# Local attention with 160 keys per 32 queries, P in DRAM rows of nine blocks, Q and K sent together

## The chip, the cores and the metric

The kernel runs on one core of a Trainium2 chip. The metric is the device time in microseconds of one execution, the median of the runs shown; the profiled execution has a time and a span of its own.

## What is computed

Two blocks follow each other. The first is an RWKV-like attention over x of shape (2, 4096, 256) (stages "mix", "scan" and "gate" of the kernel); the change does not touch it. The second, which the change touches, is a transformer of two layers with local attention. Per layer:

```
q, k, v = split(shift_token(x) @ wqkv)          # 8 heads of 64
q, k    = rotary_xpos(l2norm(q) * qs, l2norm(k) * ks)
# windows of 128 tokens, each looks at its own and the one before
sim  = (8 q) . k;   mask = (i < j) | (i > j + 128) | (j == -1)
attn = softmax(where(mask, -max, sim));  o = attn @ v
x = x + o @ wo
x = x + mlp(layernorm(shift_token(x)))          # a * gelu(g), 2 x 682 hidden
```

A query i sees the keys j with i - 128 <= j <= i, at most 129 of them. In a window of 128 queries the kernel before computes 256 scores per query, the window's own keys and those of the window before, and masks what is too far or in the future.

## The kernel before

All five engines run one long program by hand-written order and semaphores, stage after stage. `local_stage` is the last. It works in windows of P = 128 tokens. There are two batches ("streams" s = 0, 1), 32 windows each and two layers, thus units u = 0..63 per stream and 128 **halves**: `half(s, u, w, l)` does, on each engine, the attention of stream s in window u up to P (scores, softmax, transposes), and, for the other stream o, the rest of its window um (values, output projection, layer norm, MLP). w is the parity of u; it names the one of two buffers that holds the window's K and V. A head pair hp = 0..3 is two heads, which lie in partitions 0..63 and 64..127 of q and k, transposed; pairs 0, 1 are group g = 0 and pairs 2, 3 group 1.

Everything is float32. A float32 matmul shows as two MATMUL records.

**PE** (the `half` at L2582) issues per half, in this order: values of pairs 0 and 1 of the other stream (`values`, L2516), scores of pairs 0 and 1 (`scores`, L2498), values of pairs 2, 3, scores of pairs 2, 3, `project_out` (L2524), the K projection of the next window (L2473), `mean` (L2529), V projection, `variance` (L2533), Q projection, and the MLP (L2551, L2559). In layer 1 `turn_out` (L2567) stands between the first two score pairs and the second values. `scores` has two matmuls per pair, one per head: 64 rows of weights (q of 128 queries) against 256 keys. They go to PSUM banks lB and lC for an even pair, to lA of both streams for an odd one, and pairs 2 and 3 wait until VectorE has read pairs 0 and 1 (`Q["mx"]`).

**VectorE** adds the mask and takes the row maximum (`row_max`, L2186, L2193), ScalarE exponentiates (L2367), GpSimd divides by the row sum (`normalise`, L2033) and VectorE transposes P in 32x32 blocks (`turn_p`, L2202), two pairs for a write. In VectorE's order `deviate` (L2228), which subtracts the mean of the other stream's layer norm, stands ahead of `inverse_sums(s, u, 3)` and of all four `turn_p`; `turn_k` (L2158) lies between the second and the third `turn_p`, `turn_q` (L2152) near the end of the half. For window 0 of a layer the mask of the keys before is all masked; `remask` (L2213) puts it back.

**DRAM round trips.** A block transpose only turns 32x32 blocks. The blocks change places by a write to DRAM and reads back, all issued on SP's queue: `write_q` (L1891) and `read_q` (L1899), `write_k` (L1907) and `read_k` (L1915), and, per group, `write_p` (L1924) and `read_p` (L1932). A write is one transfer of 128 rows; a read is four, one for each 32 target partitions. SP's order in a half is: reads of Q, the store or load of windows, write P group 0, write K, write P group 1, read P group 0, read K, read P group 1, write Q. SP issues in this order, and each wait holds back what stands behind it. `values` of pair 2 wait for the reads of P's group 1.

```
def read_p(s, u, g):
    ...
    for j in range(BL):
        sp.dma_start(pT[s][32 * j:32 * j + 32, g].rearrange("p i h x t -> p i (h x t)"),
                     a["pz"][s, g].rearrange("(i c) (j n) -> j c i n", i=BL, j=BL)[j])...
```

In the gate stage, `load_y` reads its tokens from DRAM with the pattern `"o t c b g h i -> (o c) t (b g h i)"`, where o is 1 and c 8: 8, then 16, then 512 elements, into 128 partitions (L1524). It is not changed; the prediction counts its packets.

Of the kernel before, what the change touches and what calls it, by code (L numbers as in the profile page):

```python
# [21 lines left out]
ALU = mybir.AluOpType  # L22
# [3 lines left out]
P = 128  # L26
NB = 2
# [1718 lines left out]
def local_stage(nc, persist, a, T):  # L1746
# [7 lines left out]
    BL = P // 32  # L1754
    rows, const, ident = (persist[k] for k in ("rows", "const", "ident"))
    wqkv, wo, w1, w2, b1c, lngb, qks = (persist[k] for k in ("wqkv", "wo", "w1", "w2", "b1c", "lngb", "qks"))
    G = ((0, 1), (2, 3), (4, 5))
    with ExitStack() as ctx:
# [3 lines left out]
        wm = one("wm", [P, 2 * P])  # L1762
        mean_w, pause, least = one("mean_w", [P, P]), one("pause", [P, NB]), one("least", [P, 1])
        x1s, dsqs = two("x1s", [P, P]), two("dsqs", [P, P])
        mask = [two(f"mask{s}_", [P, 2, P]) for s in range(NB)]
# [15 lines left out]
        sems = {n: ctx.enter_context(nc.semaphore(f"l_{n}")) for n in ("wm", "set", "prep", "zero", "free", "wqkv", "wo", "w1", "w2", "wiped0", "wiped1")}  # L1781
        R = signals(nc, ctx, "tab", 1, "lr")
        S = signals(nc, ctx, "q_ps k_ps v_ps qsq ksq v_sb ss_q ss_k clamped ln_n rn rq8 kn qm qr k12 kr q_turned k_turned "
                    "q_out:16 k_out:16 qT:64 kT:64 mask0 wo_ps carry x1 x1_sum mean_ps dev dsq dsq_sum var_ps ln_v rstd hn w2_ps hout "
# [61 lines left out]
        def scored(s, hp, x):  # L1846
            return ((bank[s][1], bank[s][2]), (bank[s][0], bank[1 - s][0]))[hp % 2][x][:, 0:2 * P]
# [4 lines left out]
        with nc.Block() as block:  # L1852
            @block.sync
            def _(sp):
# [30 lines left out]
                def write_q(s, u):  # L1885
# [3 lines left out]
                    sp.wait_ge(S["qT"][s].sem, S["qT"][s].after(u, 1))  # L1889
                    sp.sem_inc(sems["free"], 1)  # L1890
                    sp.dma_start(a["qz"][s], q1[s][:].rearrange("p h d -> p (h d)")).then_inc(S["q_out"][s].sem, 16)  # L1891

                def read_q(s, u):
                    sp.wait_ge(S["q_out"][s].sem, S["q_out"][s].after(u))
                    sp.sem_inc(sems["free"], 1)
                    sp.wait_ge(Q["sc"][s].sem, Q["sc"][s].after(u * NHP - 1))
                    sp.sem_inc(sems["free"], 1)
                    for j in range(BL):
                        sp.dma_start(qT[s][32 * j:32 * j + 32].rearrange("p (i t) h -> p i (t h)", i=BL),  # L1899
                                     a["qz"][s].rearrange("(i c) (j n) -> j c i n", i=BL, j=BL)[j]).then_inc(S["qT"][s].sem, 16)  # L1900

                def write_k(s, u):
                    sp.wait_ge(S["k_turned"][s].sem, S["k_turned"][s].after(u))
                    sp.sem_inc(sems["free"], 1)
                    sp.wait_ge(S["kT"][s].sem, S["kT"][s].after(u, 1))
                    sp.sem_inc(sems["free"], 1)
                    sp.dma_start(a["kz"][s], k1[s][:].rearrange("p h d -> p (h d)")).then_inc(S["k_out"][s].sem, 16)  # L1907

                def read_k(s, u, w):
                    sp.wait_ge(S["k_out"][s].sem, S["k_out"][s].after(u))  # L1910
                    sp.sem_inc(sems["free"], 1)
                    sp.wait_ge(Q["sc"][s].sem, Q["sc"][s].after(u * NHP - 1))
                    sp.sem_inc(sems["free"], 1)
                    for j in range(BL):
                        sp.dma_start(kT[s][32 * j:32 * j + 32, w].rearrange("p i h t -> p i (h t)"),  # L1915
                                     a["kz"][s].rearrange("(i c) (j n) -> j c i n", i=BL, j=BL)[j]).then_inc(S["kT"][s].sem, 16)
# [850 lines left out]
```

## Time and profile before

| what | us |
|---|---|
| median of 3 runs (lowest, highest) | 4970.12 (4965.47, 4972.37) |
| profiled execution, its own time | 4966.22 |
| its span | 4964.4 |
| PE busy, share of the span | 4507.8, 91% |
| VectorE busy | 3564.7, 72% |
| ScalarE busy | 2979.7, 60% |
| GpSimd busy | 2441.6, 49% |
| mean granted TensorE clock | 0.959 |

An engine's busy time is the time in which at least one of its instructions runs; issuing a transfer is not counted. PE's matmuls are pipelined and their ends are modelled, so the start of the next one tells more than a length. The mean length of a matmul record holds its latency; what a record costs in a stream is busy time divided by count. For a transfer the profile gives the time from issue to landing. "SPq" is the queue on which SP issues, "PEld" the weight loads. A row's bracket tells the idle time before it and what ended it.

### The profile page before, as it was taken

Reading aid. Unit: us, or ns where it says so; the run is one execution under the profiler, and the core shown is the slowest. Engines: PE = TensorE matmul, PEld = TensorE weight load, DVE = VectorE, ACT = ScalarE, POOL = GpSimd, SP = SyncE. Lnnn points to the kernel's source line nnn. Section 1 sums busy time; section 2 is a strip of 40 time slices with the busy share of each in tenths; the row PEclk is TensorE's granted clock in tenths of the full one; section 3 lists DMA queues with packets and bytes.
Section 4 is the critical chain, followed back from the end, with each engine's and each line's share of the span. In section 5 each row is a group of like instructions: output and inputs, shape, how many; then the busy total and the mean of one; then the engine's idle time right before and its main releaser. Section 6 shows DMA issues by size and latency. Waiting matters only on the chain. (4 is left out here: it accounts for less than half of the span.)

```text
span 4964.4 us, 269505 instructions
## 1 busy us (share of the span) xinstructions
PE 4507.8 (91%) x107928; PEld 3817.4 (77%) x107928; DVE 3564.7 (72%) x10345; ACT 2979.7 (60%) x8486; POOL 2441.6 (49%) x3196
## 2 busy tenths in 40 slices
PE   7898898678888888666999999999999999999998
PEld 6888888678888888654777777777777777777777
DVE  4666666568878887475777777777777777777775
ACT  5777777534444444354666666666666666666665
POOL 1222222267777777203555555555555555555554
PEclk8999999789999999788999999999999999999999
DMA  2343343467777777694555666555565555555554
GB/s 87 87 96 93 93 98 89 114 143 165 165 165 163 167 164 161 175 299 126 170 170 168 173 174 171 172 171 171 180 196 175 173 173 172 171 171 173 173 175 131
DMA packets 1283528, 775.96 MB, mean 156 GB/s; under 512 B 686800, under 2 KB 1179088, under 8 KB 1282256
## 3 DMA queue, kind: packets, MB, share of 16 engines
q1 hardware_dynamic: 1231888, 700.43, 53.1%
q10 hardware_dynamic: 51392, 73.02, 5.0%
q14 instruction: 190, 1.56, 0.1%
q8 instruction: 58, 0.95, 0.1%
HBM read 410.44 MB, written 362.68 MB: 156 GB/s over the span
## 5 line engine op out<-in xcount | busy, mean ns | idle before, releaser
L2367 ACT ACTIVATE l_prob<-l_prob,l_nb,l_rq 128x256 f32<-128x256 f32 x1024 | 601.6, 590 | 20.8 <-DVE l_nb L2193 13.1
L2033 POOL TENSOR_TENSOR l_prob<-l_prob,l_rinv 128x512 f32<-128x512 f32 x512 | 526.8, 1039 | 108.4 <-DVE l_rinv L2173 108.4
L2017 POOL TENSOR_TENSOR l_k<-l_kn,l_tab 128x512 f32<-128x512 f32 x128 | 162.5, 1270 | 614.8 <-DVE l_kn L2165 614.8
L2559 PE MATMUL lD<-l_hid,w 128*128 128x128 f32 x3072 | 364.0, 275 | 0.0
L2559 PEld LDWEIGHTS lD<-l_hid,w 128*128 128x128 f32 x3072 | 353.3, 192 | 0.0
L2551 PEld LDWEIGHTS lA<-l_hn,w 128*128 128x128 f32 x2048 | 242.9, 195 | 110.1 <-POOL l_hn L2051 61.1
L2202 DVE STREAM_TRANSPOSE l_pb<-l_prob 128x512 f32<-128x512 f32 x512 | 326.6, 676 | 0.6 <-POOL l_prob L2033 0.5
L2027 POOL TENSOR_TENSOR l_qr<-l_q 128x512 f32<-128x512 f32 x128 | 162.4, 1269 | 328.1 <-DVE l_q L2131 328.1
L1097 POOL TENSOR_TENSOR sc_aqx<-sc_late,sc_headmask 128x256 f32<-128x256 f32 x256 | 170.8, 667 | 278.9 <-PE sc_Y L1190 277.2
L1173 PE MATMUL sc_AB<-sc_aq,sc_bkx 32*32 32x32 f32 x16384 | 257.3, 198 | 37.4 <-POOL sc_bkx L1097 29.1
L497 POOL TENSOR_TENSOR rk<-rk,bkraw 128x256 f32<-128x256 f32 x64 | 54.6, 871 | 477.9 <-DVE bkraw L383 477.9
L2551 PE MATMUL lA<-l_hn,w 128*128 128x128 f32 x2048 | 266.0, 284 | 11.8 <-POOL l_hn L2051 5.2
L1115 POOL TENSOR_TENSOR sc_bkT<-sc_tok,sc_headmask 128x128 f32<-128x128 f32 x512 | 263.2, 534 | 0.0
L2524 PE MATMUL lD<-l_oT,wo 128*128 128x128 f32 x2048 | 262.6, 281 | 0.1
L2524 PEld LDWEIGHTS lD<-l_oT,wo 128*128 128x128 f32 x2048 | 238.2, 191 | 29.2 <-issue 28.9
L2473 PE MATMUL lB<-wqkv,l_h 128*128 128x512 f32 x512 | 242.9, 597 | 17.4 <-DVE l_mask L2262 17.2
L2551 PE MATMUL lB<-l_hn,w 128*128 128x128 f32 x2048 | 250.9, 276 | 0.0
L1173 PEld LDWEIGHTS sc_AB<-sc_aq,sc_bkx 32*32 32x32 f32 x16384 | 213.3, 108 | 39.4 <-issue 38.6
L2473 PE MATMUL lC<-wqkv,l_h 128*128 128x512 f32 x512 | 241.0, 593 | 0.0
L2473 PE MATMUL lA<-wqkv,l_h 128*128 128x512 f32 x512 | 240.9, 593 | 0.0
L2551 PEld LDWEIGHTS lB<-l_hn,w 128*128 128x128 f32 x2048 | 240.5, 193 | 0.0
L2193 DVE TENSOR_TENSOR l_nb<-l_mx,l_nrq 128x2 f32<-128x2 f32 x512 | 220.6, 431 | 17.7
(276 smaller groups left out, 13707.3 us busy)
## 6 DMA issues: line engine op xcount, KB each, us to landing
scratch_pz<-l_pb SPq DMA_DIRECT2D x256, 512.0 KB, 3.0
l_pT<-scratch_pz SPq DMA_DIRECT2D x1024, 128.0 KB, 3.2
scratch_cm<-cm SPq DMA_DIRECT2D x64, 512.0 KB, 4.1
scratch_qz<-l_q SPq DMA_DIRECT2D x128, 256.0 KB, 2.9
l_qT<-scratch_qz SPq DMA_DIRECT2D x512, 64.0 KB, 2.0
scratch_kz<-l_k SPq DMA_DIRECT2D x128, 256.0 KB, 2.8
l_kT<-scratch_kz SPq DMA_DIRECT2D x512, 64.0 KB, 2.9
sc_early<-scratch_cm ACTq DMA_DIRECT2D x59, 512.0 KB, 4.7
```

What stands on the lines that cost most here:

```text
L1097: return nc.gpsimd.tensor_tensor(dst[:], src.unsqueeze(2).broadcast_to([P, 2 * BG, HQ, CH]), headmask[:].unsqueeze(1).unsqueeze(3).broadca ...
L1115: last = nc.gpsimd.tensor_tensor(bkT[c % 2][:, b * BG:(b + 1) * BG], tok[k][:, c, b, 1:3].rearrange("p x g i -> p (x g) i").unsqueeze(2) . ...
L1173: last = mm(AB_ps[c][at, (x * BG + q) * QH:(x * BG + q + 1) * QH], bkx[c][at, 2 * q + x].rearrange("p h t -> p (h t)"), aq[c][at, q], star ...
L2017: tt(k1[s][:], kn[s][:], wide(2, slice(0, DH)), ALU.mult)
L2033: tt(prob[s][:, pair], prob[s][:, pair], rinv[s][:, pair].unsqueeze(2).broadcast_to([P, 2, 2 * P]), ALU.mult).then_inc(Q["pn"][s].sem, 1)
L2193: tt(nb[s][:, pair], mx[s][:, pair], nrq8[s][:, pair], ALU.mult).then_inc(Q["nb"][s].sem, 1)
L2202: nc.vector.transpose(pb[s][:, g, :, at:at + 2].rearrange("p j h x t -> p (h x) j t"), prob[s][:, 2 * hp:2 * hp + 2].rearrange("p h (x j k ...
L2367: last_ = nc.scalar.activation(prob[s][:, h], prob[s][:, h], ACT.Exp, scale=rq8[s][:, h:h + 1], bias=nb[s][:, h:h + 1], accum_out=sums[s][ ...
L2473: last_ = mm(bank[s][j][:], h[:, k * P:(k + 1) * P], wqkv[:, k, j * INNER:(j + 1) * INNER], start=(k == 0), stop=(k == CC - 1))
L2524: last_ = mm(bank[s][3][:, m * P:(m + 1) * P], wo[:, k, m * P:(m + 1) * P], oT[s][:, k], start=(k == 0), stop=(k == NHP - 1))
L2551: last_ = mm(bank[s][j][0:MW, at:at + P], w1[:, k, tile * MW:(tile + 1) * MW], hn[s][:, k], start=(k == 0), stop=(k == CC - 1))
L2559: last_ = mm(bank[s][3][:, c * P:(c + 1) * P], w2[:, m, c * P:(c + 1) * P], hid[s][:, m], start=(c == 0 and m == 0), stop=(c == CC - 1 and ...
```

## The change

- **Scores.** Queries are taken in blocks of 32. Each block sees five blocks of 32 keys, its own and the four before it, 160 keys. `scores` has 8 matmuls per pair (4 blocks, 2 heads), each with 64x32 weights and 160 columns, into the 32 partitions of its block. For this K of the window before must lie directly ahead of K of this one: qkT has three places of four blocks; even windows use place 2 with place 1 ahead, odd windows place 1 with place 0 ahead, so the K of an even window is also read into place 0 (four more transfers, L1913 of the changed file).
- **Masks.** One mask of 160 columns per row, and one for the first window of a layer; `remask` and the mask copies at the start fall away. Row maxima, exponentials and normalisation work on 160 columns.
- **Q and K** are transposed into one buffer, written by one transfer (512 KB) and read by four of 128 KB, at the place where K was. Reads and write of Q of their own fall away.
- **P** has five blocks per row of 32 queries. Its DRAM buffer has rows of nine blocks per query block, filled with zeros once at the start; the write puts five blocks where they belong, and the reads take eight, so that the blocks that no score was made for are read as zeros. The write is 320 KB, its DRAM side is 4 x 32 x 640 elements; reads are 8 runs of 128 elements per partition where they were 4 of 256.
- On PE and SP each wait is followed by an increment of a spare semaphore (`free_pe`, `free`).
- At the start GpSimd clears qkT (3072 elements per partition) and pT (2048) for each stream where it cleared kT (1024) and a mask (256).
- The words of the change also name "deviation first on VectorE"; in the code `deviate` keeps its place between `inverse_sums` 2 and 3.

```diff
+    NR = BL + 1
+    SPAN = 32 * NR
+    PITCH = 40
...
-        qT, kT = two("qT", [P, P, NHP]), two("kT", [P, 2, BL, NHP, 32])
-        V, prob = two("V", [P, 2, HEADS, DH]), two("prob", [P, HEADS, 2 * P])
-        pb, pT = two("pb", [P, 2, BL, NHP, 2, 32]), two("pT", [P, 2, BL, NHP, 2, 32])
+        qk, qkT = two("qk", [P, BL, 2, NHP, 32]), two("qkT", [P, 3 * BL, 2, NHP, 32])
+        V, prob = two("V", [P, 2, HEADS, DH]), two("prob", [P, HEADS, SPAN])
+        pb, pT = two("pb", [P, 2, NR, NHP, 32]), two("pT", [P, 2, BL, 2, NHP, 32])
...
+                def write_qk(s, u):
...
+                    sp.dma_start(a["qkz"][s], qk[s][:].rearrange("p j y h t -> p (j y h t)")).then_inc(S["qk_out"][s].sem, 16)
...
+                def read_qk(s, u, w):
...
+                    turned = a["qkz"][s].rearrange("(i c) (j n) -> j c i n", i=BL, j=BL)
+                    cur = (2, 1)[w] * BL
                     for j in range(BL):
-                        sp.dma_start(kT[s][32 * j:32 * j + 32, w].rearrange("p i h t -> p i (h t)"),
-                                     a["kz"][s].rearrange("(i c) (j n) -> j c i n", i=BL, j=BL)[j]).then_inc(S["kT"][s].sem, 16)
+                        sp.dma_start(qkT[s][32 * j:32 * j + 32, cur:cur + BL].rearrange("p i y h t -> p i (y h t)"),
+                                     turned[j]).then_inc(S["qkT"][s].sem, 16)
+                    if w == 0:
+                        for j in range(BL):
+                            sp.dma_start(qkT[s][32 * j:32 * j + 32, 0:BL, 1].rearrange("p i h t -> p i (h t)"),
+                                         turned[j][:, :, 32 * NHP:]).then_inc(S["kT"][s].sem, 16)
...
-                    sp.dma_start(a["pz"][s, g], pb[s][:, g].rearrange("p j h x t -> p (j h x t)")).then_inc(H[g]["p_out"][s].sem, 16)
+                    n = 32 * NHP
+                    sp.dma_start(bass.AP(a["pz"].tensor, (s * 2 + g) * 32 * PITCH * n + (BL - 1) * n,
+                                         [[(2 * BL + 1) * n, BL], [PITCH * n, 32], [1, NR * n]]),
+                                 pb[s][:, g].rearrange("p r h t -> p (r h t)")).then_inc(H[g]["p_out"][s].sem, 16)
...
-                        sp.dma_start(pT[s][32 * j:32 * j + 32, g].rearrange("p i h x t -> p i (h x t)"),
-                                     a["pz"][s, g].rearrange("(i c) (j n) -> j c i n", i=BL, j=BL)[j]).then_inc(H[g]["pT"][s].sem, 16)
+                        start = (s * 2 + g) * 32 * PITCH * n + (j + BL - 1) * n
+                        sp.dma_start(pT[s][32 * j:32 * j + 32, g].rearrange("p i x h t -> p (i x) (h t)"),
+                                     bass.AP(a["pz"].tensor, start, [[PITCH * n, 32], [BL * n, 2 * BL], [1, n]])
+                                     ).then_inc(H[g]["pT"][s].sem, 16)
...
-                        for t in (kT[s], V[s]):
+                        for t in (qkT[s], V[s], pT[s]):
                             nc.gpsimd.memset(t[:], 0.0)
...
-                                                               in1=mask[s][w][:].rearrange("p x n -> p (x n)"), scale=1.0, scalar=3 * MASKED,
+                                                               in1=wm[:, int(u in (0, NW))], scale=1.0, scalar=3 * MASKED,
...
-                    for x in range(2):
-                        rows_ = slice(x * DH, (x + 1) * DH)
-                        last_ = mm(scored(s, hp, x), qT[s][rows_, :, hp], kT[s][rows_, :, :, hp].rearrange("p x i t -> p (x i) t"),
-                                   start=True, stop=True)
+                    own, back = (2, 1)[w] * BL, (1, 0)[w] * BL
+                    for i in range(BL):
+                        for x in range(2):
+                            rows_ = slice(x * DH, (x + 1) * DH)
+                            last_ = mm(scored(s, hp, x)[32 * i:32 * i + 32], qkT[s][rows_, own + i, 0, hp],
+                                       qkT[s][rows_, back + i:back + i + NR, 1, hp], start=True, stop=True)
...
-                            last_ = mm(valued(s, hp)[x * DH:(x + 1) * DH], V[s][:, slot, 2 * hp + x], pT[s][:, g, :, at + x, slot],
+                            last_ = mm(valued(s, hp)[x * DH:(x + 1) * DH], V[s][:, (1 - w, w)[slot], 2 * hp + x], pT[s][:, g, :, slot, at + x],
```

How the order of the transfers moves on SP's queue, in one half of layer 0. Before (shapes are those of the target; x4 means four in a row):

```order
L1899 DMA l_qT<-scratch_qz 32x4x128 x4
L1883 DMA scratch_h<-l_hout 256x1x128
L1861 DMA l_h_0<-scratch_h 128x2x129
L1924 DMA scratch_pz<-l_pb 128x1024
L1907 DMA scratch_kz<-l_k 128x512
L1924 DMA scratch_pz<-l_pb 128x1024
L1932 DMA l_pT<-scratch_pz 32x4x256 x4
L1915 DMA l_kT<-scratch_kz 32x4x128 x4
L1932 DMA l_pT<-scratch_pz 32x4x256 x4
L1891 DMA scratch_qz<-l_q 128x512
```

The same place after the change, in a half of the kind that also copies K (the other kind lacks L1913):

```order
L1885 DMA scratch_h<-l_hout 256x1x128
L1868 DMA l_rot<-in_rotary 128x256
L1863 DMA l_h_1<-scratch_h 128x2x129
L1923 DMA scratch_pz<-l_pb 4x32x640
L1898 DMA scratch_qkz<-l_qk 128x1024
L1923 DMA scratch_pz<-l_pb 4x32x640
L1935 DMA l_pT<-scratch_pz 32x8x128 x4
L1909 DMA l_qkT<-scratch_qkz 32x4x256 x4
L1913 DMA l_qkT<-scratch_qkz 32x4x128 x4
L1935 DMA l_pT<-scratch_pz 32x8x128 x4
```

Q's reads and write are gone from the two ends, K's place now carries both, and four transfers more stand ahead of the last reads of P. The write of P is 4x32x640 where it was 128x1024.

On PE the scores of pairs 0 and 1 and the values around them, before:

```order
L2516 MATMUL lD<-l_pT,l_V 64x128 x8
L2498 MATMUL lB<-l_kT,l_qT 128x256
L2498 MATMUL lC<-l_kT,l_qT 128x256
L2498 MATMUL lA<-l_kT,l_qT 128x256 x2
L2516 MATMUL lB<-l_pT,l_V 64x128 x8
```

and after:

```order
L2512 MATMUL lD<-l_pT,l_V 64x128 x8
L2494 MATMUL lB<-l_qkT 32x160
L2494 MATMUL lC<-l_qkT 32x160
L2494 MATMUL lB<-l_qkT 32x160
L2494 MATMUL lC<-l_qkT 32x160
L2494 MATMUL lB<-l_qkT 32x160
L2494 MATMUL lC<-l_qkT 32x160
L2494 MATMUL lB<-l_qkT 32x160
L2494 MATMUL lC<-l_qkT 32x160
L2494 MATMUL lA<-l_qkT 32x160 x8
L2512 MATMUL lB<-l_pT,l_V 64x128 x8
```

Four matmuls have become sixteen small ones; what stands around them is the same.

## Rows read from the trace of the kernel before

**Rows 1.** Windows: busy time by engine, clock, DMA share, GB/s; gate and local stage.
```profile
core 0: us, PE busy (x) PEld busy (x) DVE busy (x) ACT busy (x) POOL busy (x), PEclk, DMA share, GB/s
2100.00:2200.00 100.00, 65.21 (x304) 52.71 (x303) 70.83 (x190) 54.90 (x152) 0.00 (x0) 0.88 1.00 299
2500.00:3400.00 900.00, 897.19 (x6524) 697.66 (x6523) 667.59 (x2271) 598.36 (x1635) 492.31 (x551) 1.00 0.59 171
```

**Rows 2.** Timeline of PE and DVE, one half: start us, us, what.
```profile
3026.08 0.60 PE L2498 MATMUL lB<-l_kT,l_qT 64*128 64x256 f32 x1
...
3027.32 1.09 PE L2516 MATMUL lB<-l_pT,l_V 128*64 128x128 f32 x16
3028.34 0.60 PE L2498 MATMUL lB<-l_kT,l_qT 64*128 64x256 f32 x1
...
3029.95 2.05 PE L2524 MATMUL lD<-l_oT,wo 128*128 128x128 f32 x16
...
3033.56 0.38 PE L2529 MATMUL lD<-l_x1s,l_mean_w 128*128 128x128 f32 x2
...
3047.85 0.88 PE L2516 MATMUL lB<-l_pT,l_V 128*64 128x128 f32 x12
...
3033.98 0.42 DVE L2228 TENSOR_TENSOR l_dev<-l_x,lD 128x256 f32<-128x256 f32 x1 [1.38 <-PE lD L2529]
...
3034.39 1.28 DVE L2202 STREAM_TRANSPOSE l_pb<-l_prob 128x512 f32<-128x512 f32 x2
```

**Rows 3.** Windows of line L2524 alone, in layer 1.
```profile
3850.00:4850.00 1000.00, 98.48 (x768) 89.33 (x768) 1.00 0.59 173
```

**Rows 4.** Timeline of SP's queue, the same half.
```profile
3032.71 0.60 SPq L1861 DMA_DIRECT2D l_h<-scratch_h  x1
3035.84 0.34 SPq L1924 DMA_DIRECT2D scratch_pz<-l_pb  x1
3036.44 0.34 SPq L1907 DMA_DIRECT2D scratch_kz<-l_k  x1
3037.62 0.32 SPq L1924 DMA_DIRECT2D scratch_pz<-l_pb  x1
3038.73 1.82 SPq L1932 DMA_DIRECT2D l_pT<-scratch_pz  x4
3040.74 1.73 SPq L1915 DMA_DIRECT2D l_kT<-scratch_kz  x4
3042.64 1.74 SPq L1932 DMA_DIRECT2D l_pT<-scratch_pz  x4
```

**Rows 5.** DMA from 2600 to 3200 us; issues: count, size, us to landing.
```profile
DMA packets 102611, 101.68 MB, mean 169 GB/s; under 512 B 10544, under 2 KB 87728, under 8 KB 102576
...
q1 hardware_dynamic: 102576, 101.39, 59.2%
...
scratch_pz<-l_pb SPq DMA_DIRECT2D x59, 512.0 KB, 2.7
l_pT<-scratch_pz SPq DMA_DIRECT2D x232, 128.0 KB, 3.2
...
l_rot<-in_rotary SPq DMA_DIRECT2D x15, 128.0 KB, 2.6
```

**Rows 6.** Waits from 3000 to 4000 us: total, times, longest.
```profile
PEld lA L2498 <- DVE l_mx L2186: 10.6, 39, 0.3
...
PEld lB L2516 <- DMA l_pT<-scratch_pz: 9.9, 15, 1.6
```

**Rows 7.** Windows of L2559 and of L2516 alone; a group of the scan stage.
```profile
3000.00:4000.00 1000.00, 139.32 (x1176) 135.26 (x1176) 1.00 0.60 176
3000.00:4000.00 1000.00, 107.23 (x1568) 83.58 (x1568) 1.00 0.60 176
L1173 PEld LDWEIGHTS sc_AB<-sc_aq,sc_bkx 32*32 32x32 f32 x1586 | 20.3, 104 | 0.0
```

**Rows 8.** Timeline at the start of the local stage, POOL and PE.
```profile
2256.95 0.95 POOL L2069 MEMSET l_kT<- 128x1024 f32 x1 [225.59 <-POOLq L104]
...
2264.14 3.78 PE L2473 MATMUL lB<-wqkv,l_h 128*128 128x512 f32 x4 [17.17 <-DVE l_mask L2262]
```

**Rows 9.** DMA of the gate stage, 2103 to 2203 us.
```profile
DMA packets 28640, 30.02 MB, mean 300 GB/s; under 512 B 1683, under 2 KB 21349, under 8 KB 28640
...
ga_gr<-scratch_gr SPq DMA_DIRECT2D x19, 512.0 KB, 8.0
scratch_xa<-ga_xa SPq DMA_DIRECT2D x19, 256.0 KB, 7.8
ga_xt<-in_x SPq DMA_DIRECT2D x19, 256.0 KB, 8.0
scratch_h<-ga_h SPq DMA_DIRECT2D x38, 128.0 KB, 6.4
ga_yt<-scratch_y_tok SPq DMA_DIRECT2D x19, 256.0 KB
```

**Rows 10.** DMA from 3036.7 to 3037.9 us, within a write of P.
```profile
DMA packets 119, 0.49 MB, mean 406 GB/s; under 512 B 0, under 2 KB 0, under 8 KB 119
...
q1 hardware_dynamic: 119, 0.49, 100.9%
```

**Rows 11.** The page, part 6: issues over the whole execution.
```profile
scratch_pz<-l_pb SPq DMA_DIRECT2D x256, 512.0 KB, 3.0
```

More of the change, by code:

```diff
@@ L1761, in local_stage @@
         rot, tab = two("rot", [P, 4, DH]), two("tab", [P, 4, DH])
-        wm = one("wm", [P, 2 * P])
+        wm = one("wm", [P, 2, SPAN])
         mean_w, pause, least = one("mean_w", [P, P]), one("pause", [P, NB]), one("least", [P, 1])
         x1s, dsqs = two("x1s", [P, P]), two("dsqs", [P, P])
-        mask = [two(f"mask{s}_", [P, 2, P]) for s in range(NB)]
         hT = [two(f"h{s}_", [P, CC, P + 1]) for s in range(NB)]
@@ L1940, in first @@
                     sp.dma_start(wm[:], a["winmask"]).then_inc(sems["wm"], 16)
[L1941 to L1945 removed]
+                    sp.wait_ge(sems["set"], 1)
+                    for s in range(NB):
+                        for g in range(2):
+                            sp.dma_start(a["pz"][s, g], pT[s][:].rearrange("p g i x h t -> p (g i x h t)")[:, 0:PITCH * NHP * 8]
+                                         ).then_inc(sems["blank"], 16)
+                    write_qk(0, 0)
+                    read_qk(0, 0, 0)
+                    sp.wait_ge(sems["blank"], 16 * 2 * NB)
                 def half(s, u, w, l, mlp=True):
@@ L2181, in row_max @@
                     dve.wait_ge(Q["p_turned"][s].sem, Q["p_turned"][s].after(n, NHP))
-                    if hp == 0 and w == 0:
-                        dve.wait_ge(S["mask0"][s].sem, S["mask0"][s].after(u, 1))
                     nc.vector.memset(pause[:, s:s + 1], 0.0)
@@ L2259, in first @@
                     dve.wait_ge(sems["set"], 1)
-                    for s in range(NB):
-                        nc.vector.tensor_copy(mask[s][0][:, 0, :], wm[:, P:2 * P])
-                        last = nc.vector.tensor_copy(mask[s][1][:].rearrange("p x n -> p (x n)"), wm[:])
-                    last.then_inc(sems["prep"], 1)
-                    dve.wait_ge(sems["prep"], 1)
                     for s in range(NB):
@@ L2587, in half @@
                     if mlp:
-                        values(o, um, 0, layer(um, l))
-                        values(o, um, 1, layer(um, l))
+                        values(o, um, wm_, 0, layer(um, l))
+                        values(o, um, wm_, 1, layer(um, l))
                     scores(s, u, w, 0)
@@ L2594, in half @@
                     if mlp:
-                        values(o, um, 2, layer(um, l))
-                        values(o, um, 3, layer(um, l))
+                        values(o, um, wm_, 2, layer(um, l))
+                        values(o, um, wm_, 3, layer(um, l))
                     scores(s, u, w, 2)
@@ L2624, in last @@
                     for hp in range(NHP):
-                        values(s, u, hp, 1)
+                        values(s, u, w, hp, 1)
                     turn_out(1 - s, u)
@@ L2707, in lay_out @@
     out["eye16"] = np.ascontiguousarray(np.broadcast_to(np.eye(CH, dtype=np.float32), (P, 2, CH, CH)))
-    q, kx = np.arange(P)[:, None], np.arange(P)[None, :]
-    neg = np.float32(MASKED)
-    before, own = np.where(kx < q, neg, 0), np.where(kx > q, neg, 0)
-    out["winmask"] = np.concatenate([before, own], axis=1).astype(np.float32)
+    row, r = np.arange(P)[:, None], np.arange(160)[None, :]
+    neg, behind = np.float32(MASKED), r - row % 32
+    near = np.where((behind < 0) | (behind > P), neg, 0)
+    begin = np.where(r < P - row // 32 * 32, neg, near)
+    out["winmask"] = np.stack([near, begin], axis=1).astype(np.float32)
     n = out["x"].shape[1]
```

90 lines of the change are left out of this document (34 added, 56 removed).

## The prediction

> **What bounds the kernel now.** I read the windows by stage first. In the local stage (from about 2260 us to the end, 2.7 of the 4.96 ms, and the only stage that the change touches) PE is busy over 99% of the time at granted clock 1.00, with DVE at 74%, ACT at 66%, POOL at 55% and DMA at 59% [rows 1]. So PE bounds this stage, or something lies so close behind it that PE hardly waits. The timeline of one half shows which. On PE the values of head pairs 2 and 3 (L2516, to lB) start at 3027.32 and in the next half at 3047.85 [rows 2]: a half takes 20.5 us in layer 0. In layer 1, 768 records of L2524, 16 to a half, in 1000 us make 20.8 us [rows 3].
>
> Then I follow what those values wait for, the chain that goes through DRAM. Values at 3027.32, scores of pairs 2 and 3, L2524, a projection, the mean at 3033.56; DVE's deviation at 3033.98 and, behind it on DVE, the transposes of P at 3034.39; SP's first write of P at 3035.84, the K write, the second write of P at 3037.62, four reads of P, four of K, and the four reads of group 1 of P from 3042.64 on [rows 2, 4]. The last of those four is issued near 3044.0 and lands a median 3.2 us later [rows 5], at about 3047.2; PE wants it at 3047.85. **This loop has about 0.6 us of slack in 20.5.** The waits agree: PE's weight load for these values already waits for the DMA 15 times in 1000 us, 9.9 us in all [rows 6]. Two loops thus run almost level, PE's own and the one through DRAM, and the change touches both.
>
> **The change, part by part.**
>
> Scores. A head pair has now 2 matmuls of 64x128 weights and 256 columns; after it has 8 of 64x32 and 160. Now two pairs take 1.24 us (3026.08 to 3027.32) and the second two 1.61 us (3028.34 to 3029.95), of which part is the wait for the row maxima, 10.6 us in 39 cases of 1000 us [rows 2, 6]. The trace has no 64x32 tile. Below: a record of 128 columns costs 139.32/1176 = 118 ns at full array [rows 7], so 160 columns cost 0.15 us, two records per matmul 0.3 us, if all eight tiles run side by side. Above: the four column groups in turn, 1.2 us per pair. The nearest row is L2516, where two 64-column tiles over the same 128 rows make 1568 records in 107.23 us, 68 ns each [rows 7]: column groups that share rows do run side by side. I take 0.4 us per pair, thus 0.8 for pairs 2 and 3 (minus 0.8) and 0.8 for pairs 0 and 1 (minus 0.4). The added waits' increments lie under queued matmuls; I cost them at nothing.
>
> A rule speaks against this part: the Trainium skill ("TensorE: Matmul & The Clock Gate", Part 3) says that a weight load overlaps running matmuls only when its row group differs. By it 16 loads of 104 ns [rows 7] would take 1.7 us per pair. L2516's loads, same rows throughout, are busy 83.58 us under those 107.23, so this trace disagrees and I keep 0.4.
>
> Vector work. Two transposes of P take 1.28 us [rows 2]; at 320 instead of 512 elements 0.4 us less per two. The masked row maxima, exponentials, POOL's normalisation and the mask copy shrink too; they lie beside PE, and only the first pair of transposes stands between the deviation and the first write. The deviation itself stays where it was in VectorE's order: the change's words name it, its code does not move it.
>
> Q and K. One write of 512 KB and four reads of 128 KB replace two writes of 256 KB and eight reads of 64 KB. In every second half four more reads of 64 KB copy K, and they stand ahead of the reads of P's group 1. A read costs SP 0.43 us [rows 4], so these halves put group 1 off by 1.7 us, more than its slack. Q's reads ahead of the store and load go away; they were early and hide nothing.
>
> Start. POOL clears 3072 + 2048 elements per stream where it cleared 1024 and the mask: at 0.95 us per 1024 [rows 8] about 7 us more in all. PE, which started at 2264.14 behind the mask copies, starts near 2269: **plus 5 us**, once. The blanking of P in DRAM is over before the first transposed Q is ready.
>
> **The write of P** is the term that decides. Now it is 128 rows of 4 KB on both sides, and the order shows 128x1024. After it is 4x32x640: its DRAM side has an outer dimension of 4. How a transfer spreads over the 16 engines can be counted. From 2600 to 3200 us the transfers that SP issues add up to 659 (nine kinds, 59 of the first and 15 of the last), and there are 10544 packets under 512 B, though no data run is that short: 16.0 per transfer, one completion per engine [rows 5]. In the gate stage 95 transfers of four kinds and 19 of L1524 leave 1683 such packets; 95 x 16 = 1520, so L1524 has 163/19, about 8 [rows 9]. L1524 is the one transfer there with an outer dimension of 8 on its DRAM side ((o c) = 8 rows, then 16, then 512 elements) against 128 partitions. So eight outer rows get eight engines, and I expect 4x32x640 to get four. The Trainium skill ("DMA: Bandwidth & Descriptors", Why a DMA increments its semaphore by 16 and not by 1) says the same in general: the number of engines is the largest up to 16 that divides the outermost dimension of both sides. The reads keep 32 partitions outermost and stay on 16.
>
> Each of the four engines then carries 32 rows of 2560 B, 80 KB. In a burst of the present write all 16 engines are busy at 100.9% with 119 packets of 4 KB in 1.2 us: 25 KB per us and engine [rows 10]. That gives **3.3 us of engine time per write**, where it is 1.3 now. Over the local stage the mean is 101.39 MB at 59.2% of 16 engines in 600 us, 17.8 KB per us [rows 5], the other bound: 4.5 us. I take 3.3 for writes (same kind as the burst) and 1.8 for each 32 KB per engine of short reads (the mean rate). The write also becomes an issue of the kind of L1861, 0.60 us against 0.34 [rows 4].
>
> **The sum, around the loop.** Write of group 0 now issued at 3035.84 - 3027.32 = 8.5; minus 0.8 (scores), minus 0.4 (transposes): 7.3. First packet: a 512 KB write lands after a median between 2.7 [rows 5] and 3.0 us [rows 11], of which 1.3 are transfer, so 1.6 is fixed, by my estimate 0.9 ahead and 0.7 behind; with 0.3 for the longer issue the first packet is at 8.5. Now the four loaded engines work their queue in order: P group 0 3.3, the Q and K write 1.3, P group 1 3.3 (16.4), reads of group 0 1.8, of Q and K 1.8, of group 1 1.8 (21.8), landing 0.7: 22.5. In every second half K's copy adds 0.9: 23.4. Mean **22.95 us per half**. PE's own loop shrinks to about 19.5 and no longer binds; it would idle 3.4 us per half ahead of the values and of the scores. Against 20.5 in layer 0 (64 halves): plus 157. Against 20.8 in layer 1 (63): plus 135. With the start: 4966.2 + 297 = 5263, on the profiled execution, which stands 4 us under the median of 4970.1. I say 5265. Bounds: reads at the burst rate as well (1.3 each) give 21.3 per half and 5055; writes at the mean rate (4.5, 1.8, 4.5) give 25.9 and 5630, which the burst row speaks against.
>
> **Rivals.**
> - The write of P goes over 16 engines after all. For it: 659 transfers of the local stage all do. Against: L1524. Its time: PE's loop is 19.5 and 19.8. P's group 0 is issued at 7.6 and landed at 10.0; 11 further issues of 0.44 and a landing of 3.2 bring group 1 at 18.0, and 15 issues, with K's copy, at 19.8. That is a mean of 19.65 in layer 0 and 19.8 in layer 1: minus 54, minus 63, plus 5: 4854, faster. It decides from eight engines on (1.6 us a write hides under 20.5). Chance 0.08.
> - Four engines, but it costs little: reads and writes all above 25 KB per us and engine, a half of 20.2 to 20.7: 4914 to 4978. Chance 0.04.
> - Scores in turn by column group, or loads in turn as the page's rule says, on top of the forecast: pairs 2 and 3 take 2.4 instead of 0.8 and the loop gains 1.6: plus 203, 5466. For it: nothing in the trace has four column groups over the same rows. Against: L2516. Chance 0.07.
> - PE idles 15% of each half and its clock falls. At 65% busy the granted clock is 0.88 in the gate stage [rows 1]. At 0.93, the 5.5 us of PE in the loop grow by 0.4: plus 50, 5315. Chance 0.08.
>
> **How the numbers follow.** The forecast keeps 0.73. About 0.2% is what a measurement of this kernel can tell from no change. Slower: 0.73 + 0.07 + 0.08 = 0.88; of the low-cost case half is within 0.2%: same 0.02; faster 0.10. The range takes in the low bound, 5055, and reaches up to 5520 for scores in turn together with writes somewhat under the burst rate; it leaves out the first two rivals and the far end of the third.
>
> **What would show each step.** Packets under 512 B: a half has two P writes, so four engines show as (16 - 4) x 2 = 24 fewer completions than 16 per transfer. The P write lands in about 4.5 us or more where it is 2.7 to 2.9. PE's weight loads for L2516's successor wait for l_pT in nearly every half, 2 us or more, and PE is busy near 85%. SP waits long for the P write's landing ahead of its reads. A pair of scores takes 0.4 us from its first record to its last start. PE's first local matmul comes near 2269. The prediction is wrong if the P write lands in under 3 us, or if PE's waits for l_pT stay in tenths of a us.

## The result, and the profile after

| | before | after |
|---|---|---|
| median (lowest, highest), us | 4969.24 (4965.47, 4972.37) | 6053.13 (6049.22, 6061.19) |
| profiled execution, its span, us | 4966.22, 4964.4 | 6061.19, 6059.4 |
| mean granted clock | 0.959 | 0.866 |

The change makes the kernel slower, by a ratio of 1.2184 (95% interval 1.2163 to 1.2205). The forecast was 5265, its range ended at 5520: the sign was right, and the size was off by 788 us, some 6 us in every half. One execution of the kernel before took 6522 us and one of the kernel with all local scores 12209; the medians and ratios below leave these two out.

The windows of the local stage after, and of the line of the output projection (now L2520, 16 records to a half) in both layers, answer to [rows 1, 3].

```profile
core 0: us, PE busy (x) PEld busy (x) DVE busy (x) ACT busy (x) POOL busy (x), PEclk, DMA share, GB/s
2500.00:3400.00 900.00, 680.85 (x6076) 517.97 (x6076) 391.37 (x1581) 401.96 (x1147) 302.62 (x385) 0.84 0.42 110
...
2500.00:3400.00 900.00, 71.48 (x496) 65.57 (x496) 0.84 0.42 110
...
3850.00:4850.00 1000.00, 78.28 (x560) 71.61 (x560) 0.84 0.44 117
```

31 halves in 900 us are 29.0 us each in layer 0, 35 in 1000 us are 28.6 in layer 1, where there were 20.4 and 20.8. PE is busy 76% where it was over 99%, every other engine has less to do, and the DMA engines are busy 42% instead of 59%. Nothing is full, so something is waited for in turn. The waits say what (totals from 3000 to 4000 us, times, longest):

```profile
PE lD L2512 <- DMA l_pT<-scratch_pz: 213.3, 34, 7.3
...
PEld lB L2512 <- DMA l_pT<-scratch_pz: 24.6, 27, 1.3
```

34 halves in that stretch, each with a wait of 6.3 us for P's **group 0** (to lD). The forecast had the wait at group 1 (to lB), which is the small one. One half, on PE (clock 0.50, 0.68 and then 1.00 by the windows under it; 0.50 and 1.00 are its two levels, 1.2 and 2.4 GHz) and on SP's queue:

```profile
3613.03 1.97 PE L2512 MATMUL lD<-l_pT,l_V 128*64 128x128 f32 x16 [6.65 <-DMA l_pT<-scratch_pz]
...
3617.13 1.84 PE L2512 MATMUL lB<-l_pT,l_V 128*64 128x128 f32 x16 [0.58 <-DMA l_pT<-scratch_pz]
...
3619.61 2.05 PE L2520 MATMUL lD<-l_oT,wo 128*128 128x128 f32 x16
...
3641.31 1.98 PE L2512 MATMUL lD<-l_pT,l_V 128*64 128x128 f32 x16 [6.21 <-DMA l_pT<-scratch_pz]
...
3645.38 1.97 PE L2512 MATMUL lB<-l_pT,l_V 128*64 128x128 f32 x16
```

```profile
3613.00:3617.10 4.10, 3.30 (x48) 2.29 (x48) 0.94 (x8) 0.37 (x1) 0.00 (x0) 0.50 0.49 127
3617.10:3619.60 2.50, 2.47 (x48) 2.03 (x48) 0.63 (x7) 0.58 (x2) 0.00 (x0) 0.68 0.01 2
3619.60:3627.20 7.60, 7.60 (x40) 4.35 (x32) 5.50 (x24) 5.93 (x21) 4.38 (x7) 1.00 0.13 24
```

```profile
3625.11 0.57 SPq L1923 DMA_DIRECT2D scratch_pz<-l_pb  x1
3626.21 0.35 SPq L1898 DMA_DIRECT2D scratch_qkz<-l_qk  x1
3626.76 2.32 SPq L1923 DMA_DIRECT2D scratch_pz<-l_pb  x1
3633.05 2.58 SPq L1935 DMA_DIRECT2D l_pT<-scratch_pz  x4
3635.98 1.73 SPq L1909 DMA_DIRECT2D l_qkT<-scratch_qkz  x4
3639.21 1.78 SPq L1935 DMA_DIRECT2D l_pT<-scratch_pz  x4
```

From the values of pairs 2 and 3 at 3617.13, P's first write is issued 7.98 us later, the reads of group 0 can only go out at 15.9 (7.94 after their write's issue, where it was 2.89, [rows 4]), PE has group 0 at 24.2, and the next values of pairs 2 and 3 start at 28.25.

### The profile page after: what moved, and what is told of

Read it like the earlier page. It is cut to its first block and busy times, and to the rows that moved or that the text cites. A ratio compares the mean times of both kernels' runs of the same rounds, so it can differ in the third digit from the quotient of the medians.

```text
span 6059.4 us, 281812 instructions
## 1 busy us (share of the span) xinstructions
PE 4713.3 (78%) x114072; PEld 3926.1 (65%) x114072; DVE 3211.6 (53%) x10277; ACT 2900.3 (48%) x8486; POOL 2283.5 (38%) x3196
## 2 busy tenths in 40 slices
DMA packets 1356818, 745.21 MB, mean 123 GB/s; under 512 B 677648, under 2 KB 1268240, under 8 KB 1355536
## 5 line engine op out<-in xcount | busy, mean ns | idle before, releaser
L2512 PE MATMUL lD<-l_pT,l_V 128*64 128x128 f32 x2048 | 251.6, 426 | 787.8 <-DMA l_pT<-scratch_pz 787.8
L2035 POOL TENSOR_TENSOR l_prob<-l_prob,l_rinv 128x320 f32<-128x320 f32 x512 | 362.7, 718 | 1157.6 <-DVE l_rinv L2175 1157.6
L2186 DVE CUSTOM_DVE_ANT_0 l_prob<-lB,l_wm 128x160 f32<-128x160 f32 x256 | 81.9, 320 | 1289.0 <-issue 1284.6
L2512 PEld LDWEIGHTS lD<-l_pT,l_V 128*64 128x64 f32 x2048 | 200.7, 223 | 812.6 <-DMA l_pT<-scratch_pz 482.8
L2352 ACT ACTIVATE l_prob<-l_prob,l_nb,l_rq 128x160 f32<-128x160 f32 x1024 | 521.5, 514 | 14.2 <-DVE l_nb L2193 14.2
L2361 ACT COPY l_oT<-lD 128x256 f32<-128x256 f32 x128 | 47.8, 373 | 991.3 <-PE lD L2512 991.3
L2520 PEld LDWEIGHTS lD<-l_oT,wo 128*128 128x128 f32 x2048 | 264.7, 209 | 49.3 <-issue 37.4
L2361 ACT COPY l_oT<-lB 128x256 f32<-128x256 f32 x128 | 47.8, 374 | 506.4 <-PE lB L2512 506.4
L2520 PE MATMUL lD<-l_oT,wo 128*128 128x128 f32 x2048 | 289.1, 298 | 0.1
L2494 PE MATMUL lB<-l_qkT 64*32 64x160 f32 x2048 | 186.5, 439 | 102.6 <-DMA l_qkT<-scratch_qkz 74.4
L2512 PE MATMUL lB<-l_pT,l_V 128*64 128x128 f32 x2048 | 245.6, 419 | 22.2 <-DMA l_pT<-scratch_pz 21.9
```

The source lines that it names most:

```text
L2035: tt(prob[s][:, pair], prob[s][:, pair], rinv[s][:, pair].unsqueeze(2).broadcast_to([P, 2, SPAN]), ALU.mult).then_inc(Q["pn"][s].sem, 1)
L2352: last_ = nc.scalar.activation(prob[s][:, h], prob[s][:, h], ACT.Exp, scale=rq8[s][:, h:h + 1], bias=nb[s][:, h:h + 1], accum_out=sums[s][ ...
L2494: last_ = mm(scored(s, hp, x)[32 * i:32 * i + 32], qkT[s][rows_, own + i, 0, hp], qkT[s][rows_, back + i:back + i + NR, 1, hp], start=True ...
L2512: last_ = mm(valued(s, hp)[x * DH:(x + 1) * DH], V[s][:, (1 - w, w)[slot], 2 * hp + x], pT[s][:, g, :, slot, at + x], start=(slot == 0), s ...
L2520: last_ = mm(bank[s][3][:, m * P:(m + 1) * P], wo[:, k, m * P:(m + 1) * P], oT[s][:, k], start=(k == 0), stop=(k == NHP - 1))
```

## Experiments

Line numbers differ a little between these kernels; names and tiles don't. A time from a single execution is marked *. Executions of one kernel lie up to some 14 us apart (5383.15 to 5396.82 in one case), so a difference between two single ones is good to about that.

| kernel | us |
|---|---|
| changed kernel | 6053 |
| P's writes split in four, group 0 / 1 / both | 5810* / 5739* / 5395 |
| both split, K's copy behind group 1's reads | 5286* |
| the same, Q and K apart | 4954* |
| changed kernel, Q and K apart | 5799* |
| the same, K's copy late | 5734* |
| before, its P write as 4x32x1024 | 6350* |
| before, its P writes split in four | 5053* |

**Four engines or not.** The write of P, cut into four transfers to the same addresses:

```diff
-                    sp.dma_start(bass.AP(..., [[(2 * BL + 1) * n, BL], [PITCH * n, 32], [1, NR * n]]), pb[s][:, g]...)
+                    for i in range(BL):
+                        sp.dma_start(bass.AP(..., [[PITCH * n, 32], [1, NR * n]]), pb[s][32 * i:32 * i + 32, g]...)
```

> The changed kernel, but each write of P goes out as four transfers of 32 partitions to the same addresses: same bytes, same rows of 2560 B, same pitch, only the outer dimension of each transfer is 32. Theory spread (the one transfer with an outer dimension of 4 sits on four DMA engines): the writes land in about 3 us, packets under 512 B come to 16 per transfer, the half falls from 28.7 us to about 21 to 22 (three more issues of 0.4 us per write on SP's queue remain), the whole near 5080 us (4950 to 5200). Rival pitch (short rows far apart in DRAM are what is slow): nothing changes, 6000 us or more.

Measured 5394.87, ratio to before 1.0848 (1.0826 to 1.087): 658 us gone with the same bytes in the same rows. The page of the changed kernel and that of the split one count the completions:

```profile
DMA packets 1356818, 745.21 MB, mean 123 GB/s; under 512 B 677648, under 2 KB 1268240, under 8 KB 1355536
```

```profile
DMA packets 1372180, 745.29 MB, mean 138 GB/s; under 512 B 693008, under 2 KB 1283600, under 8 KB 1370896
```

693008 - 677648 = 15360 = 256 x 60. Each of the 256 writes has 64 completions when split (4 x 16), so it had **4** before: four engines, exactly. (That a split write has 64 is seen in a stretch of its trace: from 2600 to 3200 us, 643 transfers have 10276 such packets, 16.0 each.) The rule cited in the prediction (the Trainium skill, "DMA: Bandwidth & Descriptors", Why a DMA increments its semaphore by 16 and not by 1) gives this number; by it, too, the issuing sequencer adds the missing 12 counts at once. No run here shows that second part. The time is above the 4950 to 5200 of the expectation: two more costs were left in it, below.

The cost alone, in the kernel before: a gap of one row behind each 32 rows in DRAM, so that the two outer dimensions can't merge.

```diff
-                    sp.dma_start(a["pz"][s, g], pb[s][:, g]...)
+                    sp.dma_start(bass.AP(a["pz"].tensor, ..., [[33 * 1024, BL], [1024, 32], [1, 1024]]), pb[s][:, g]...)
```

> The kernel before, its write of P with a gap of one row in DRAM after every 32 rows, so that the transfer is 4x32x1024 and nothing else changes. Theory spread: each of four engines carries 128 KB, 5.2 us at the burst rate, per write; two writes and the reads behind them give a half of 29 to 32 us, the whole 6100 to 6400 us; 24 packets under 512 B fewer per half. Rival pitch (or any other part of the change is to blame): within 1% of 4970.

Measured 6350. SP's queue, one half:

```profile
3612.47 0.59 SPq L1924 DMA_DIRECT2D scratch_pz<-l_pb  x1
3613.25 0.36 SPq L1907 DMA_DIRECT2D scratch_kz<-l_k  x1
3614.18 1.24 SPq L1924 DMA_DIRECT2D scratch_pz<-l_pb  x1
3623.73 1.74 SPq L1933 DMA_DIRECT2D l_pT<-scratch_pz  x4
```

The reads follow their write by 11.3 us instead of 2.9 [rows 4]. A gap in DRAM behind every 32 rows, which the reads step over, costs 1380 us with nothing else changed. The rival that short rows or their pitch are slow is out as the main cause: the split kernel keeps both and loses 658 us, and this one has rows of 4 KB, side by side but for the gap.

**Which of the two writes.**

> Only the write of group 0 is split in four, group 1's stays one transfer. Theory spread: group 0 lands in about 3 us, but its reads queue behind group 1's write on the four engines, so the values of pairs 0 and 1 still wait; a half about 24 to 25 us, the whole 5350 to 5550. Rival pitch: 6050. If only the landing of group 0 counted, the time would be that of the kernel with both split.

> Only the write of group 1 is split in four. Theory spread: group 0's write still lands in 5 us or more, its reads go out late, but queue behind nothing; a half about 25 us, the whole 5400 to 5650. If the queue behind group 1's write were all, the time would be that of the kernel with both split.

Measured 5810 and 5739: 243 and 314 us, together 557 of the 658. Neither is enough by itself. I had expected 5350 to 5550 and 5400 to 5650: with one write still on four engines a half takes 27 us, more than the sum of transfers gave me, for the same reason as in the forecast (below).

**What a split costs, and the place of K's copy.**

> The kernel before with each write of P issued as four transfers of 32 partitions: same bytes to the same addresses. It prices the issues alone. Theory (SP's issues stand in the loop): six more issues of 0.34 to 0.43 us ahead of group 1's reads are 2.0 to 2.6 us, less 0.6 of slack: a half of about 22.1 to 22.5 us, the whole 5150 to 5230 us. Rival (issues are hidden, landing is what counts): within 1% of 4970.

Measured 5053, plus 84 us: 0.7 us per half for six more issues, not 2.0. SP's queue, one half:

```profile
3605.50 1.91 SPq L1925 DMA_DIRECT2D scratch_pz<-l_pb  x4
3607.63 0.34 SPq L1907 DMA_DIRECT2D scratch_kz<-l_k  x1
3608.16 1.80 SPq L1925 DMA_DIRECT2D scratch_pz<-l_pb  x4
3610.14 1.79 SPq L1934 DMA_DIRECT2D l_pT<-scratch_pz  x4
```

The two writes take 3.7 us to issue where they took 0.7, 3.0 us more. Of these, 1.3 went into the gaps of SP's queue ahead of the second write and of the reads (0.84 and 0.79 us in [rows 4], 0.19 and 0.18 here), which I had not counted as slack, and 0.6 into the slack. That is nearer to the 0.7 measured, and 0.4 us are left open.

> The changed kernel with P's writes split in four, and with the four transfers that copy K issued behind the reads of P's group 1 instead of ahead of them. Theory (SP's issues stand in the loop): every second half gains up to 1.8 us, 64 x 1.8 = 115 us at most: 5280 to 5340 us where both splits gave 5395. Rival (the halves wait for Q and K instead): no change, 5380 to 5400.

Measured 5286: 109 us, near the most that it could be. With split writes SP issues without a gap from the first write of P to the last read, and an issue moved out of that row is worth its whole time in every second half.

**Q and K.** In the last kernel PE still waits, for Q and K first (3000 to 4000 us):

```profile
PE lB L2501 <- DMA l_qkT<-scratch_qkz: 73.0, 43, 2.1
PE lB L2519 <- DMA l_pT<-scratch_pz: 44.1, 41, 1.9
```

So Q and K were sent apart again, in two transfers of 256 KB and reads of 64 KB, Q's at its old place; PE's and vector work stay.

```diff
-                        write_qk(o, un)
+                        write_k(o, un)
...
-                        read_qk(o, un, wn)
+                        read_k(o, un, wn)
...
+                    if within(u + 1):
+                        write_q(s, u + 1)
```

> The kernel with P's writes split and K's copy late, and Q and K sent apart again as before (Q's write and reads at the ends of the half, K's where Q and K were). Theory (SP's 21 issues ahead of the last reads are what the half waits for, and they stay 21): PE's wait for Q and K turns into a wait for P's group 1, 5200 to 5290 us where it was 5286. Rival (the larger transfer of Q and K is the cost): 5050 to 5150 us.

My theory failed: 4954, minus 332 us. SP's row of 21 issues is as long as before, and it hardly matters. What the merging did is to put Q's way through DRAM, which had been over long before, into the stretch in which everything is waited for: from 3000 to 4000 us no wait of PE is for Q's transfers any more, and 1.9 us are for K's. The run changes the place of Q's transfers and the size of those in K's place together; what each of the two is worth isn't shown. In the changed kernel itself:

> The changed kernel with Q and K sent apart again; P's writes stay one transfer of 4x32x640 and K's copy stays ahead of group 1's reads. It says what the merging of Q and K costs in the changed kernel itself, after it was 332 us in the kernel without the four-engine writes. Theory (there it made PE wait for Q and K ahead of the scores and lowered PE's clock; here PE waits for P anyway): the four engines carry 32 KB each less between the two writes of P, 1.3 to 1.9 us per half at most half of it: 0.6 to 2 us a half, the whole 5800 to 5980 us. Rival (merging costs its 330 us here too): 5700 to 5750.

Measured 5799, just under the range that I expected: 254 us for the merging. With K's copy moved as well, the four engines alone are left:

> The changed kernel with Q and K apart and K's copy behind group 1's reads, so that against the kernel of 4954 us only P's writes differ: two transfers on four engines instead of eight on sixteen. It prices the four engines alone. Theory (the four engines are the cause of most of it, whatever else is in the kernel): 5700 to 5800 us, the copy's place worth less than 0.5 us per half there, since the last reads of P wait for the write of group 1 and not for SP. Rival (the parts add up: 5799 less the 109 that the copy's place gave with split writes): 5690 or less.

Measured 5734: the copy's place is worth 65 us there, and the four engines 5734 - 4954 = 779. In this order the change falls into 254 + 65 + 779; in the other into 658 + 109 + 332. The 779 and the 658 are net of the six more issues that the split kernels have. Both end at 4954: what remains of the change (160 columns, short rows, split writes) is a little faster than the kernel before, 15 us by one execution.

**The clock.** Two kernels keep PE at work with matmuls of no use while it would wait. The first is the changed kernel with

```diff
                         out(o, um, 2)
+                        for _ in range(6):
+                            mm(bank[o][2][:], ident[:], rows[:, 0:512], start=True, stop=True)
```

> The changed kernel with six matmuls of 128 by 512 columns put at the end of each half, into a bank that nobody reads then: 5.2 us of PE's time at full clock, where PE idles 6 to 9 us for the reads of P. The work is of no use; nothing else is changed. Theory (PE's idling lowers its clock, and the values and scores behind the wait, which the loop through DRAM goes through, then run at half speed: 6.6 to 7.2 us from the first values to the output projection, where a kernel with the same scores and no idling takes 4.0): with PE kept at work the clock stays high, 2 to 2.6 us of each half go, the whole 5720 to 5800 us with more PE work in it. Rival (the clock is a bystander, the loop waits for transfers alone): 6050 us or more.

Measured 5991.88, ratio 1.2062 (1.2042 to 1.2083): faster than the changed kernel, with more work, but by 61 us and not by 250. Its timeline of PE:

```profile
3623.64 5.32 PE L2618 MATMUL lC<-rows,ident 128*128 128x512 f32 x12
3630.03 1.09 PE L2512 MATMUL lD<-l_pT,l_V 128*64 128x128 f32 x16 [1.08 <-DMA l_pT<-scratch_pz]
3632.81 0.44 PE L2494 MATMUL lB<-l_qkT 64*32 64x160 f32 x1 [1.68 <-DMA l_qkT<-scratch_qkz]
```

The first values take 1.09 us instead of 1.97, and PE then waits for Q and K instead. From the first values to the second it is 4.03 us here (3630.03 to 3634.06) and 4.07 to 4.10 in the changed kernel. The fall of the clock is real, and most of it is hidden by the next transfer. The second, on the kernel with split writes and K's copy late, has two such matmuls ahead of the scores and one ahead of the values of pairs 2 and 3. They overwrite V's projection before it is read, so its values are computed from other numbers; the instructions are the same.

> The kernel with P's writes split and K's copy late (5286 us), with three matmuls of 128 by 512 columns of no use: two between the values of pairs 0 and 1 and the scores, one ahead of the values of pairs 2 and 3, where PE idles 1.7 and 1.3 us per half. It says how much of the 332 us that sending Q and K apart gave back is PE's clock. Theory (the merged Q and K cost a wait of about 1.7 us, and the idling then halves the clock in the stretch that P's write waits for): the wait stays, the clock returns, a half loses 0.8 to 1.2 us, 5130 to 5190 us. Rival (the clock is a bystander here too): 5270 to 5340. Rival (all of it is clock): 4950 to 5050.

Measured 5182.82, ratio 1.0427 (1.0408 to 1.0445), granted clock 1.00 in the local stage where it was 0.95. It is 1.00 in the kernel with Q and K apart as well, so at least 103 of the 332 us are clock. How the other 229 divide stays open: PE is busy 894 of 900 us in this kernel, so its own 2.6 us of added work per half (half of the six matmuls' 5.3) now hold it.

**A version that beats both.** The scores' new form is worth having alone. On the kernel before, with two matmuls where the slots stand in reverse order:

> The kernel before with the local scores alone: per block of 32 queries a matmul of 64x32 weights over its 160 keys, put at the columns of the 256 that the mask leaves open (in windows with the slots in reverse order two matmuls, over own and over earlier keys); layouts, vector work and transfers are those of before. Theory (scores of small tiles run side by side, two pairs in 0.7 us where they took 1.24 and 1.61): PE's loop loses about 1.4 us of 20.5, the loop through DRAM about 0.9, a half takes about 19.2 to 19.6 us, the whole 4810 to 4860 us. Rival (column groups in turn, or the weight loads of the same rows do not overlap): slower than 4970.

Measured 5038.63, ratio 1.0139 (1.0122 to 1.0156): slower, though some halves take 19.9 us, and far from the 4810 to 4860 that I expected. 7 times in 1000 us (3000 to 4000) PE stops ahead of the values for nothing that the profile shows, up to 3.9 us. The first five stops are 85 us apart, which is the length of the loop's body of four halves, and the last two 88. Behind six of the seven the 16 records of the values take 1.17 to 1.88 us instead of 1.09. The seven stops add up to 24.8 us in the 1000; how the rest of the loss comes about isn't shown. Instruction packets are up as well, 98 where the kernel before has 24:

```profile
PEld lD L2530 <- issue: 24.8, 7, 3.9
```

```profile
q8 instruction: 98, 1.61, 0.7%
```

With local scores in odd windows only (48 more matmuls per four halves and not 160):

> The kernel before with local scores in the windows of odd parity alone, where one matmul per block of queries and head does; even windows keep their two matmuls per pair. It has 48 matmuls more per four halves where the kernel with local scores in all windows has 160 more. Theory (that kernel's stall of about 3 us per four halves on PE, for nothing that the profile shows, comes with the length of PE's code): the stall is gone, q8's packets of instructions fall from 98 per 1000 us to about 24, and the shorter scores of half the windows show: 4880 to 4950 us. Rival (the stall belongs to the small matmuls themselves): 4970 to 5010.

Measured 4934.15, ratio 0.9931 (0.9918 to 0.9945), q8 at 29 packets. Then K in three places in order of time, as the change has it, so that one matmul does in every window, and all else as before:

> Local scores in all windows with one matmul per block and head: K in three places in order of time with its copy behind group 1's reads, the matmuls of block i put at columns 32 i to 32 i + 159, masks of two kinds instead of the remade one; P (256 columns, one write of 128x1024 per group), vector work, and Q and K apart as before. It has 96 matmuls more per four halves. Theory: no stall for code (as the kernel with P split and Q apart, which has the same PE work and shows none), PE's loop about 19.1 us, the loop through DRAM about 19.9: 4850 to 4900 us. Rival (the loop through DRAM does not move, or code stalls come back): 4930 to 5040.

> The kernel with local scores in all windows once more, unchanged: 4895 to 4910 us, 0.984 to 0.988 of before.

Measured 4900.62 (three executions) and 4900.27, ratio 0.986 both times (0.984 to 0.988; 0.9842 to 0.9877): 69 us faster than the kernel before, at the price of 96 matmuls more per four halves, an extra copy of K on a free place of the queue, and no change to P. It fell short of its 4850 to 4900 by a little: PE is busy 875 of 900 us. Its own waits are small: 10.0 us per 1000 for row maxima, 9.6 for P's group 1, 4.9 for the variance of the layer norm. (The weight loads wait 44.8 us for that variance, but nearly all of it lies under running matmuls.)

```profile
3016.16 1.09 PE L2529 MATMUL lD<-l_pT,l_V 128*64 128x128 f32 x16
...
3017.91 1.09 PE L2529 MATMUL lB<-l_pT,l_V 128*64 128x128 f32 x16
...
3020.14 2.05 PE L2537 MATMUL lD<-l_oT,wo 128*128 128x128 f32 x16
```

## Why the prediction was wrong, step by step

- **Two loops run level, the one through DRAM will bind.** Right. PE's waits are for l_pT.
- **The write of P goes over four engines.** Right, exactly four, from the counting of completions; it is the largest part, 658 to 779 us. The rival with 16 engines is out.
- **3.3 us of engine time per write, from the burst of [rows 10].** This term failed. In the trace's packet records the 8746 packets of 2560 B between 3400 and 4400 us have a median of 102 ns, which is the burst's 25 KB per us, but a mean of 144: 32 of them are 4.6 us. Likewise 8 packets of 4 KB of the write between them take 1.9 us and not 1.3. So the mean rate of the stage, which I had as the far bound (4.5, 1.8, 4.5, a half of 25.9 and 5630 us) and of which I said that the burst row speaks against it, was nearer. It isn't enough for the landing. In the half above, the completions of the four engines come 4.43, 4.47, 5.23 and 6.22 us after the write's first packet, where the sum had all four at 3.3, and SP issues the reads 0.5 us behind the last of them. Few packets make the difference: of the first 128, which is one write, 10 take over 0.3 us each, and they hold 5.0 of the 7.0 us that the 128 take beyond 102 ns each. What slows these packets isn't shown. The order on the engines (P group 0, Q and K, P group 1) was as forecast: on each of the four in this half, Q's and K's packets follow the completion of group 0.
- **The loop goes through group 1, and PE follows at once.** This step failed too. Group 0's reads queue behind group 1's write on the same four engines and arrive at 24.2, not at 18.9, and the values of pairs 0 and 1, two pairs of scores and their waits (4.1 us at clock 0.50, and 1.75 in the last timeline above at 1.00) come after that. I had checked only the last of the waits, not what PE must still do behind the first. In numbers per half: 0.7 for a later issue of the first write (values and scores below full clock), 2.7 for its own landing (3.3 of engine time against the 6.2 of the slowest engine), 1.9 for the second write and the reads, and 0.5 because PE needs 4.1 us from there where the forecast's second group came 3.6 later: 22.5 becomes 28.3. The halves with K's copy add the rest to 29.0.
- **Q's reads ahead were early and hide nothing.** Wrong, and not in the sum at all: 254 to 332 us. Merged with K they land in the stretch that P's transfers fill, 3.6 us after each issue in the changed kernel and 3.3 with split writes, where Q's took 2.0 and K's 2.5 in the kernel with both apart, and PE waits for them as soon as P is less late.
- **K's copy adds 0.9 us in every second half.** 65 us in this place (1.0 us per such half), 109 with split writes. The size was right.
- **Scores at 0.4 us per pair.** Right: two pairs take 0.73 us at full clock (3017.18 to 3017.91 in the kernel with all local scores).
- **PE idles and its clock falls, 0.4 us per half.** It falls to 0.50 behind the wait, where the loop's own work is, and not to 0.93 evenly: from 3000 to 4000 us no record of the values behind it is under 421 ns, where one takes 272 at full clock. What it is worth was near my guess: 61 us, or 0.5 us per half. That is luck: the fall is deeper than I had it, and the next transfer hides most of it.
- **Plus 5 us at the start.** Right: from the first memset to PE's first matmul 11.6 us, before 7.2 [rows 8]. The matmul comes at 2273.59 and not near 2269, because the first memset, too, is 5.0 us later (2261.98) in this execution.

## What to carry to other kernels

A write whose outermost DRAM dimension is 4 uses four DMA engines, and everything later on the queue that touches these four waits behind it: look at the outermost dimension of both sides before the bytes. When such a burst is priced, take the mean rate of the stage rather than that of an undisturbed burst and add something for the slowest of the engines (4.6 us by the mean and up to 6.2 here), follow the first of the arrivals that an engine needs and not only the last, and add what the engine does behind it at the clock that it then has. And a transfer that is early isn't free to move: look at the stretch that it lands in after the move.

## What the runs showed of the hardware

- Behind a wait of 6 us PE runs at half clock for a few us: 16 records of the same values take 1.97 us instead of 1.09. Behind two waits of 1.8 and 1.2 us, in the kernel with split writes and the late copy, they took 1.98 as well, but in its next half, behind waits of 1.5 and 1.6, they took 1.09.
- Four engines with equal shares of one write (32 packets of 2560 B each) aren't done together: 4.4, 4.5, 5.2 and 6.2 us after the first packet in the half shown. In the other halves from 3410 to 4400 us the first is done after 4.2 to 4.6 us and the last after 5.3 to 6.0.
- A kernel with a longer loop of PE code has stops of about 3 us: the one with 160 more matmuls per four halves has them, those with 96 and 48 do not, and instruction packets on q8 are 98 per 1000 us with it and 32 and 29 without (24 in the kernel before). That the reload of code is the cause is argued from these numbers and from the edit; it wasn't tested by itself, and the kernel with the stops is also the only one with two matmuls per block in the windows of reverse order.
- SP took 2.32 us to issue the second four-engine write, and 1.75 in the half before, where the first took 0.57, and 0.32 to 0.34 in the kernel before [rows 4].
